# Cutting the gather loads of a down projection into four transfers, and one wait ahead of an output projection in place of sixteen

## The reference

```python
x = L0_attn_Q_input                                   # (4, 4096, 2048) f32
x = _layernorm(x + _L0_attn_ref(x, Wq, Wk, Wv, Wo))   # H = 16, HD = 128
x = _layernorm(x + _L0_ffn_ref(x, w_gate, w_up, w_down))

# attention
Q = (Q_input @ Wq).reshape(b, s, H, HD);  K = Q_input @ Wk;  V = Q_input @ Wv
scores = jnp.einsum('bshd,btd->bhst', Q, K) * SCALE
attn = jax.nn.softmax(scores, axis=-1)
out = jnp.einsum('bhst,btd->bshd', attn, V).reshape(b, s, H * HD) @ Wo

# feed-forward, hidden width 8192
gated = jax.nn.silu(x @ w_gate.T) * (x @ w_up.T)
out = gated @ w_down.T
```

## Time and profile before

| | us |
|---|---|
| median of 2 runs (6610.67 and 6624.28) | 6617.48 |
| the profiled execution | 5955.31 |
| its span, from the first instruction to the last (core 4) | 5953.7 |
| spans of the 8 cores | 5839.2 to 5953.7 |
| TensorE busy | 4961.9 (83%) |
| ACT busy | 1368.5 (23%) |
| DVE busy | 710.8 (12%) |
| granted TensorE clock, mean of core 4 | 0.925 |

### The profile page before, as it was taken

How to read it: one execution, slowest core, us unless ns; L and a number is a source line. 1 busy time by engine, 2 the same in 40 slices (tenths; PEclk the granted TensorE clock), 3 DMA queues, 4 the chain that set the end, 5 groups by cost and what they waited for, 6 DMA issues and landing times.

```text
span 5953.7 us, 65352 instructions; the slowest of 8 cores (5839.2 to 5953.7 us)
## 1 busy us (share of the span) xinstructions
PE 4961.9 (83%) x27328; PEld 2523.4 (42%) x27328; DVE 710.8 (12%) x1027; ACT 1368.5 (23%) x1514; POOL 135.1 (2%) x255
## 2 busy tenths in 40 slices
PE   3999988997998899678999989999977766667771
PEld 2862242224223222433444434444446655556651
DVE  0221112112111211200000000000000000000011
ACT  0016635663663566200000000000000000000012
POOL 0000010001000000100000000000000000000000
PEclk8999997998999999899999999999988888888885
DMA  8110033006002300632223242322238787787793
GB/s 134 29 33 1 1 57 85 1 1 139 3 1 45 97 1 1 144 60 63 57 50 64 45 81 52 64 47 60 64 82 219 225 227 205 212 211 198 219 290 132
DMA packets 290287, 550.59 MB, mean 92 GB/s; under 512 B 48848, under 2 KB 145104, under 8 KB 270288
## 3 DMA queue, kind: packets, MB, share of 16 engines
q1 hardware_dynamic: 218144, 304.15, 17.7%
q0 software_dynamic: 23984, 177.23, 16.6%
q10 hardware_dynamic: 47872, 65.03, 3.5%
HBM read 608.21 MB, written 90.18 MB: 117 GB/s over the span
## 4 chain that ended last, share of the span: by engine, by line
PE 63%; DMA 22%; SPq 7%; ACT 2%; DVE 2%; issue 2%; another core or an unknown queue 1%; ACTq 1%; POOL 0%; DVEq 0%; POOLq 0%
DMA RB<-gat_hbm 13%; PE stB L676 11%; PE stA L667 10%; PE sr L431 9%; PE ho L423 8%; SPq L705 6%; PE stA L469 5%; PE stB L469 4%; DMA gat_hbm<-RE 3%; PE ho L803 3%; PE sr L803 3%; DMA RC<-r_hbm 3%; DMA RC<-wo_h 2%; PE stA L353 2%; PE stB L353 2%
## 5 line engine op out<-in xcount | busy, mean ns | idle before, releaser
L676 PE MATMUL stB<-RB,RC 128*128 128x512 bf16 x4096 | 930.3, 381 | 95.0 <-DVE RE L695 95.0
L667 PE MATMUL stA<-RB,RD 128*128 128x512 bf16 x4096 | 930.2, 381 | 46.6 <-ACT RE L686 33.2
L676 PEld LDWEIGHTS stB<-RB,RC 128*128 128x128 bf16 x4096 | 399.1, 98 | 589.3 <-issue 115.0
L667 PEld LDWEIGHTS stA<-RB,RD 128*128 128x128 bf16 x4096 | 398.4, 98 | 527.0 <-issue 52.7
L486 ACT ACTIVATE PTB<-stA 128x1024 bf16<-128x1024 f32 x512 | 524.0, 1023 | 417.0 <-PE stA L469 417.0
L423 PE MATMUL ho<-PTB,RE 128*128 128x512 bf16 x2048 | 618.9, 384 | 0.0
L431 PE MATMUL sr<-PTB,ONE 128*1 128x512 bf16 x2048 | 614.0, 381 | 0.0
L486 ACT ACTIVATE PTB<-stB 128x1024 bf16<-128x1024 f32 x512 | 523.7, 1023 | 191.2 <-PE stB L469 191.2
L686 ACT ACTIVATE RE<-stA 128x512 f32<-128x512 f32 x256 | 152.7, 597 | 1713.0 <-PE stA L667 1434.3
L803 PE MATMUL ho<-RA,RB 128*128 128x256 bf16 x2816 | 342.3, 288 | 183.4 <-DMA RB<-gat_hbm 170.9
L803 PE MATMUL sr<-RA,RB 128*128 128x256 bf16 x2688 | 319.2, 284 | 133.3 <-DMA RB<-gat_hbm 133.3
(11 more groups left out here) (79 smaller groups left out, 2197.2 us busy)
## 6 DMA issues: line engine op xcount, KB each, us to landing
RC<-wo_h POOLq DMA_DIRECT2D x32, 1024.0 KB, 10.4
RD<-wg_h POOLq DMA_DIRECT2D x32, 1024.0 KB, 9.0
RC<-wu_h POOLq DMA_DIRECT2D x32, 1024.0 KB, 14.0
gat_hbm<-RE SPq DMA_DIRECT2D x256, 128.0 KB, 12.8
RA<-wd_h POOLq DMA_DIRECT2D x8, 4096.0 KB, 32.8
RC<-xt_h POOLq DMA_DIRECT2D x16, 1024.0 KB, 9.8
RA<-xn_h POOLq DMA_DIRECT2D x128, 128.0 KB, 5.0
y1f_hbm<-RA SPq DMA_DIRECT2D x16, 1024.0 KB, 8.7
```

What stands on the lines that cost most here:

```text
L667: (lambda i=i, j=j, g=g, tc=tc, gb_off=gb_off: (lambda e: e.matmul(stA[:, gb_off:gb_off + 512], wg_ap(g % 2, i * 256 + j * 128, i * 256 + ...
L676: (lambda i=i, j=j, g=g, tc=tc, gb_off=gb_off: (lambda e: e.matmul(stB[:, gb_off:gb_off + 512], wu_ap(g % 2, i * 256 + j * 128, i * 256 + ...
```

## The change

1. **Gather loads in D2.** Each load of 64 rows `ht` becomes four transfers of 16 rows each, issued by SP one behind the other after the same wait as before, into the same places. Each quarter has its own semaphore for each of the two buffers, eight in place of two. TensorE waits for quarter `ht // 16` ahead of the matmuls with `ht` = 0, 16, 32 and 48, in both halves `tsub`, in place of one wait ahead of each half.
2. **Waits in phase C.** The sixteen waits for `s_hoevac` inside the first group of each chunk's output projection, and the one after its second group, go; one wait for all sixteen heads of the chunk stands ahead of the projection.

Nothing else is changed: the amount of data, the matmuls and the other waits are the same. The diff without the list of semaphore names:

```diff
@@ -500,6 +502,7 @@
         emit_rep(qc * 16 + 15)
         emit_repc(qc * 16 + 15)
         r.w("tensor", "s_exp", (qc + 1) * 256)
+        r.w("tensor", "s_hoevac", (qc + 1) * 16)
         attrot = [stA[:, 0:256], stA[:, 512:768], stB[:, 0:256], stB[:, 512:768]]
         for dc in range(8):
             gw = qc * 8 + dc
@@ -508,10 +511,7 @@
                 g_att = qc * 32 + dc * 4 + qt
                 ab = attrot[g_att % 4]
                 r.w("tensor", "s_r1v", g_att - 3)
-                first_grp = (dc == 0 and qt == 0)
                 for f in range(16):
-                    if first_grp:
-                        r.w("tensor", "s_hoevac", qc * 16 + f + 1)
                     r.do("tensor",
                          (lambda f=f, qt=qt, qc=qc, gw=gw, ab=ab: (lambda e: e.matmul(
                              ab,
@@ -519,8 +519,6 @@
                              wo_ap(gw % 2, f * 256, (f + 1) * 256),
                              start=(f == 0), stop=(f == 15))))(),
                          "s_att" if f == 15 else None)
-                if dc == 0 and qt == 1:
-                    r.w("tensor", "s_hoevac", (qc + 1) * 16)
                 r.w("vector", "s_att", g_att + 1)
                 r.w("vector", "d_xn%d" % (g_att % 4), 16 * (g_att // 4 + 1))
                 r.do("vector",
@@ -765,13 +763,14 @@
                 r.w("sync", "sD1_g", 32)
             else:
                 r.w("sync", "s_down", (pos_g - 1) * 2)
-            r.do("sync",
-                 (lambda tc2=tc2, par_g=par_g: (lambda e: e.dma_start(
-                     AP(RB, par_g * 16384,
-                        [[32768, 128], [256, 64], [1, 256]]),
-                     AP(gat_hbm, tc2 * HTN * 32768,
-                        [[256, 128], [32768, 64], [1, 256]]))))(),
-                 "d_gr%d" % par_g, 16)
+            for q in range(4):
+                r.do("sync",
+                     (lambda tc2=tc2, par_g=par_g, q=q: (lambda e: e.dma_start(
+                         AP(RB, par_g * 16384 + q * 4096,
+                            [[32768, 128], [256, 16], [1, 256]]),
+                         AP(gat_hbm, tc2 * HTN * 32768 + q * 16 * 32768,
+                            [[256, 128], [32768, 16], [1, 256]]))))(),
+                     "d_gr%dq%d" % (par_g, q), 16)
             gat_loads.append((par_g, gl // 2 + 1))
         par_g, grcnt = gat_loads[-1]
         for tsub in range(2):
@@ -794,10 +793,11 @@
                                  dcq * 256:(dcq + 1) * 256])))(),
                      "d_y1c%d" % (j % 4), 16)
             r.w("tensor", "d_wd%d" % (dc % 2), 16 * (dc // 2 + 1))
-            r.w("tensor", "d_gr%d" % par_g, 16 * grcnt)
             r.w("tensor", "s_r2v", pos - 5)
             db = rot[pos % 6]
             for ht in range(HTN):
+                if ht % 16 == 0:
+                    r.w("tensor", "d_gr%dq%d" % (par_g, ht // 16), 16 * grcnt)
                 r.do("tensor",
                      (lambda ht=ht, dc=dc, tsub=tsub, par_g=par_g, db=db:
                       (lambda e: e.matmul(
```

More of the change, by code:

```diff
@@ L77 @@
     "d_y1f0", "d_y1f1",
-    "d_y1b0", "d_y1b1", "d_y1T0", "d_y1T1", "d_y1T2", "d_y1T3", "d_gw0", "d_gw1", "d_gr0", "d_gr1",
+    "d_y1b0", "d_y1b1", "d_y1T0", "d_y1T1", "d_y1T2", "d_y1T3", "d_gw0", "d_gw1",
+    "d_gr0q0", "d_gr0q1", "d_gr0q2", "d_gr0q3",
+    "d_gr1q0", "d_gr1q1", "d_gr1q2", "d_gr1q3",
     "d_y1c0", "d_y1c1", "d_y1c2", "d_y1c3", "d_r2w0", "d_r2w1", "d_r2w2",
```

## The result

The changed kernel takes 5801 us at the median of 11 runs, and 0.9745 of the kernel before (95% interval 0.9712 to 0.9778): 2.55% faster. The forecast of the direction holds, the forecast 6467 us and its range (6405 to 6625) do not.

What follows compares the result with a forecast made beforehand. D2 was taken as bound by whole gather loads alternating with whole matmul groups. 110 + 18.6 - 6.8 = 122 us off 5955.3 gave 5833; carried to the median 6617 with saving 151, the forecast was 6467 us, range 6405 to 6625.

Steps and rivals of the forecast that it cites:

- the last of the sum: Whole kernel: carried the saving from the profiled execution (5955.3 to 5833 us) to the median 6617, giving 6467 us.
- two ways: Reading the 662 us: DMA-bound part as in the trace, saving 122 us; or slower matmuls, saving 180; middle 151.
- The stretch to the second landing: D2, start of a `dc` until both first gather loads and `wd_h` are in: stays at 62 us.
- A load in a full queue: D2, SP's queue never empties: each gather load takes 17.5 us, five more 87.5; bounds 15.8 and 20.9.
- The tail: D2, 80 matmuls left after the last piece: 9.6 us, from 8.7 to some 10.5, instead of 15.9 to 16.9.
- A `dc`: D2: 62 + 87.5 + 9.6 = 159.1 us instead of 177.5, 18.4 less; six save 110 us.
- The first `dc`: D2: six more loads and the tail end at 4570.6 instead of 4589.2 us, 18.6 us less.
- The last `dc`: D2, from about 5655 us: bound by `r_hbm` loads and ACT's and DVE's work; length unchanged, moves forward as a whole.
- Phase C: Output projection's one wait starts each first group 1.7 us later, 4 x 1.7 = 6.8 us lost; bounds 0 and 14.
- Rival 1: SP's queue in D2: joins between pieces lose some 1.6 us each, kernel slower, about 6725 us; decides at 0.9; chance 15%.
- Rival 2: D2: small transfers set the rate, 19 us a load, a `dc` 166.6 us, saving 68 us in all: 6549; chance 15%.
- Rival 3: D2: short waits keep TensorE's clock low, a group takes 21 us, a `dc` 177: no change, 6620 us; chance 10%.

Runs made afterwards that it cites:

- `sixteen_pieces`: Changed kernel with each gather load in sixteen transfers of 256 KB instead of four of 1 MB, same four semaphores and waits; a `dc` took 165.6 us against 153.7.

## Why the prediction was wrong, and what in it was right

**The step that failed is the last of the sum.** "The median is 6617, 662 us longer than that, and no row says where": from there I carried the saving over to 6617 and took the middle of two ways. The sum on the profiled execution's own time was 5833 us; the changed kernel's profiled execution took 5779, its median 5801. Forty-five executions of the unchanged kernel are on record by now, from 5905 to 6651 us, and the 6617 is the middle of two long ones. Their clocks were not recorded, but the seven others beyond 6500 us all show one die at a granted clock of 0.78 to 0.83; in one of 6604 us its cores have spans of 6449 to 6602 us, and those of the other die, at 0.93, 5832 to 5876. So the 662 us were very likely slower matmuls, as one of the two ways had it, and what failed was to take that time as the starting point. A range that covered both would have had to begin near 5760, which the text had worked out and turned into 6403. As a ratio the forecast was 0.977 (6467 of 6617), and 0.9745 was measured.

**The mechanism held; two of its sizes were off.**
- The stretch to the second landing: 62 us taken, 60.9 measured (44.6 + 16.3).
- A load in a full queue: 17.5 taken, 16.60 measured. This is one mis-sized term. The pair of the earlier trace rows was a queue that started from empty and ran out, and I spread its start and run-out over two loads, although in the walk it happens once in a `dc`. The kernels with a quarter of the work showed 15.8 to 16.0, near the lower bound I had worked out from the busy shares (15.8).
- The tail: 9.6 taken. By the trace it is 8.91 us at the full clock, and of 261 tails that begin when the last piece lands 40 had a lowered clock and took 10.6 on the mean. The end gap of 9.7 holds 0.7 us more than the tail.
- A `dc`: 18.4 us forecast, 19.6 measured on the mean of the cores (21.9 between the slowest cores' 177.5 and 155.6). That 18.4 and 19.6 lie so close is in part luck: the 159.1 us forecast were for core 4, which measured 151.5, and its 177.5 before were 4.2 above the mean of the cores.
- The first `dc`: 18.6 forecast, 24.0 measured (166.9 to 142.9), counted from the first load's issue; the 17.5 stood in it six times.
- The last `dc`: left as it was, and measured so: from the sixth load of `wd_h` to the end 476.8 became 456.1, 20.7 less, of which 19.8 are `dc` 6 (174.1 to 154.3); the last `dc` itself took 302.7 and then 301.8.
- Phase C: 6.8 us taken, 10.9 measured at the 33rd matmul, within its bounds of 0 and 14. This is the other mis-sized term: 2.0 us of the 2.7 at each place stand before the first matmul, and the rest goes with the granted clock, 0.58 against 0.67 up to the 33rd, as the upper bound there had it.
- Together 122 forecast, 146.5 measured on the mean span. Of D2 alone 128.6 were forecast and 143.0 measured; the rest lies ahead of D2, where 6.8 us more were forecast and the pair of profiles shows 3.5 less, for no reason that the change gives.

**The rivals.** Rival 1: a join costs 0.12 us by `sixteen_pieces`, not 1.6; its break-even was 0.9. The sag at the join of two whole loads wasn't the price of a join. Rival 2: small transfers cost 0.84 us each beside gather loads, more than their own share, but the load's 16.6 us include that. Rival 3: the granted clock in D2 rose to 0.91 to 0.93, from 0.84 to 0.86, core by core. Yet short waits can lower it: after idle times of 2.0 us two tails above had 10.57 us in place of 8.91, where the earlier trace rows, read as harmless, had shown 128 matmuls at the full clock after 2.31. The fixed 2.0 us of the Trainium skill ("DMA: Bandwidth & Descriptors", "Anatomy of one DMA", measured there on GpSimd's path) aren't paid for each piece in SP's queue when it is filled: twelve more transfers cost a load 1.44 us.

**What is open.** Why twelve joins cost 1.4 us while the engines are nearly as busy as before (on core 4 SP stays in its issues for 145 of the 165 us of a `dc` with sixteen pieces, for 119 of 151 with four; no run separates this from the transfers); why the second load takes 1.3 us more in the changed kernel; and why a load takes 16.60 us there and 16.01 with a quarter of the matmuls.

## What to carry to other kernels

Where a chain alternates whole transfer and whole computation through two buffers, cut the wait and not just the transfer: the gain here was the part of the computation that no longer stands behind the last piece, as far as the queue could use the buffer that came free. Price it by the queue that is full afterwards, not by one that starts and runs out, and look for the next idle stretch (here the reload at a `dc`'s end, worth a further 7.7 us of 153.7) and for the rows' size (11 us). Before forecasting a time, ask why the timed executions differ from the profiled one (here by 662 us); until that is known, forecast the saving or the ratio (0.977 against 0.9745), not the time.

## What the hardware showed that I had not expected

- An issue on SP's queue behind running transfers stays for 3 to 4 us (3.46 at the median in one `dc`), and the piece lands 10 to 13 us after it (11.7 at the median), though it is a quarter of a load and a quarter takes 4.1 us. So about three pieces are under way or queued at once. It is no fixed lead: on core 4, pieces of 256 KB landed 5.9 us after their issue and pieces of 2 MB 18.4 us, at the median. How far ahead a load must be issued for the queue to stay filled, no run shows.
- Rows of 512 bytes against 8 KB: 16.60 and 14.65 us for 4.2 MB, 102 and 85 us of DMA time in a `dc`.
- A 128 KB transfer beside these loads makes a `dc` 0.84 us longer, where its own share of the engines is 0.48 us.
- Of 261 tails in the changed kernel 40 ran with a lowered clock and took 10.6 us in place of 8.9; in the kernel before, of 181 groups that began when their load landed, 160 ran their first 80 matmuls with a lowered clock, in 10.9 us.
